# Last block of a two-layer hybrid network: scan's rows transposed between two products, masks signalled by chunk, last pass added and stored by halves

## The reference

```python
x = x + _L1_ffn_ref(_layernorm(x), w_gate, w_up, w_down)
x = x + _L1_attn_b_ref(_layernorm(x), W_act, W_val, W_rec)
x = x + _L1_ffn_ref(_layernorm(x), w_gate, w_up, w_down)

def _L1_ffn_ref(x, w_gate, w_up, w_down):
    h = silu(x @ w_gate) * (x @ w_up)            # 1024 wide
    h_sparse = _sparsify_2to4(h)                 # of each 4 neighbours the 2 largest in magnitude stay
    return h_sparse @ w_down

def _L1_attn_b_ref(x, W_act, W_val, W_rec):      # "the scan"
    ct = concat([x shifted by one row, x])       # 512 wide
    z = sigmoid(relu(ct @ W_act.T))              # 256 numbers, read as 128 complex ones
    z = z / cummax(|z|)                          # running maximum over the rows
    kv = running complex product of z over the rows
    r = sigmoid(relu(ct @ W_rec.T))
    return (kv @ W_val.T) * r ** 4
```

## Time and profile before

| | |
|---|---|
| median of 3 runs | 1644.63 us (1636.43 to 1647.76) |
| the profiled execution's own time | 1641.78 us |
| its span, first to last instruction | 1639.7 us |
| TensorE matmuls busy | 1398.7 us, 85% of the span |
| VectorE busy | 1049.0 us, 64% |
| ScalarE busy | 625.2 us, 38% |
| GpSimd busy | 295.8 us, 18% |
| mean granted clock of TensorE | 0.924 of full |
| bytes moved by DMA | 42.00 MB, mean 26 GB/s |

### The profile page before, as it was taken

The page is one execution under the profiler, slowest core; times in us unless marked ns, Lnnn a source line. Parts: engine busy times, 40 slices in busy tenths (PEclk is TensorE's granted clock), DMA queues, the critical chain, the costliest instruction groups (busy, mean ns, idle before and its releaser), DMA issues. The chain is left out here.

```text
span 1639.7 us, 21649 instructions
## 1 busy us (share of the span) xinstructions
PE 1398.7 (85%) x8144; PEld 1002.1 (61%) x8144; DVE 1049.0 (64%) x2056; ACT 625.2 (38%) x1160; POOL 295.8 (18%) x251
## 2 busy tenths in 40 slices
PE   3799999857999877799976899898879979889897
PEld 2455555446888766688864444343257767677676
DVE  5555555187887456778746556666256568888775
ACT  1254544342333212333321455656632323433321
POOL 0210000044433200243331320200040200120010
PEclk9799999578999988999996799999989989999899
DMA  8615220040000000000015404110000000000000
GB/s 190 87 27 79 44 37 2 1 149 1 1 1 1 1 0 1 0 1 1 1 39 73 75 27 75 27 24 1 1 0 1 1 1 1 0 1 1 13 13 26
DMA packets 23063, 42.00 MB, mean 26 GB/s; under 512 B 4705, under 2 KB 6497, under 8 KB 22833
## 3 DMA queue, kind: packets, MB, share of 16 engines
q1 hardware_dynamic: 22960, 40.64, 13.2%
HBM read 14.54 MB, written 2.10 MB: 10 GB/s over the span
## 5 line engine op out<-in xcount | busy, mean ns | idle before, releaser
L1312 DVE TENSOR_REDUCE attn_negm<-ps 128x2 f32<-128x1024 f32 (+3 forms) x256 | 256.2, 1021 | 115.5 <-PE ps L940 57.4
L1160 ACT ACTIVATE attn_probs<-ps 128x512 f32<-128x512 f32 (+3 forms) x512 | 237.0, 515 | 188.9 <-PE ps L973 112.0
L480 POOL TENSOR_TENSOR moe_h_low<-moe_h,moe_h_high 128x512 fp32r<-128x512 f32 x96 | 139.8, 1458 | 328.8 <-ACT moe_h_high L430 328.8
L964 PE MATMUL ps<-attn_qs,attn_ks 64*128 64x512 f32 (+3 forms) x512 | 154.9, 418 | 38.1 <-ACT attn_probs L1160 35.4
L447 ACT ACTIVATE moe_silu<-ps 128x512 f32<-128x512 f32 x96 | 57.4, 598 | 228.0 <-PE ps L353 227.9
L940 PE MATMUL ps<-attn_ks,attn_qs 63*128 63x512 f32 (+3 forms) x512 | 120.9, 469 | 26.6 <-DMA attn_ks<-attn_part_low 21.5
L964 PEld LDWEIGHTS ps<-attn_qs,attn_ks 64*128 64x128 f32 x512 | 72.1, 193 | 102.7 <-ACT attn_probs L1160 97.9
L1683 PE MATMUL ps<-sb_f_down,tail_h 128*128 128x256 f32 x512 | 123.3, 387 | 7.1 <-DVEq L1976 7.1
L988 PE MATMUL ps<-attn_probs,attn_va 128*32 128x512 f32 (+3 forms) x1024 | 123.8, 559 | 0.0
L1683 PEld LDWEIGHTS ps<-sb_f_down,tail_h 128*128 128x128 f32 x512 | 98.5, 193 | 24.0 <-DVEq L1976 7.3
L940 PEld LDWEIGHTS ps<-attn_ks,attn_qs 63*128 63x128 f32 x512 | 51.9, 199 | 93.8 <-issue 62.4
(11 more groups left out here) (319 smaller groups left out, 3281.2 us busy)
## 6 DMA issues: line engine op xcount, KB each, us to landing
attn_qs<-attn_part_high SPq DMA_DIRECT2D x64, 128.0 KB, 4.9
attn_qs<-attn_part_low SPq DMA_DIRECT2D x32, 128.0 KB, 4.5
attn_ks<-attn_part_high SPq DMA_DIRECT2D x32, 128.0 KB, 6.1
attn_ks<-attn_part_low SPq DMA_DIRECT2D x16, 128.0 KB, 7.0
out_x<-x SPq DMA_DIRECT2D x4, 512.0 KB, 2.6
x<-in_x SPq DMA_DIRECT2D x1, 1536.0 KB, 12.9
attn_qs<-attn_mT SPq DMA_DIRECT2D x64, 4.0 KB
moe_raw<-in_f_gate SPq DMA_DIRECT2D x2, 512.0 KB, 6.3
```

The costliest lines, as they stand in the source:

```text
L480: pool.tensor_tensor(hc.low[:, j % RING, :], h[:, j % RING, :], hc.high[:, j % RING, :], ALU.subtract).then_inc(low_done, 1)
L964: last = pe.matmul(ps[:, SC + k, 0:width2(kt)], ks[e:e + ROWS2, b % 2, key_tile(hd), kt * P:(kt + 1) * P], qs[e:e + ROWS2, b % 2, hd // 2, ...
L1160: act.activation(pr[:, s2 % RING, j, 0:n], ps[:, SC + k, 0:n], ACT.Exp, scale=HD ** -0.5).then_inc(exp_done, 1)
L1312: dve.tensor_reduce(m, ps[:, 2 * half:2 * half + 2, 0:width1(qt)], AX, ALU.max, negate=True).then_inc(r1_free, 1)
```

## The change

Four edits, all in the last block.

1. **The scan's rows.** TensorE transposes the rows of entry b in slot s + 2 between `chunk(s + 2)` and `down(s - 5)`; before it did so at the end of slot s + 1. ScalarE's two copies move from the jobs of slot s + 1 to those of slot s + 2. The table `pe_between` is new. Banks stay as they were, since no other job of banks 6 and 7 lies in between.
2. **Masks by chunk.** `sel_done` and the instruction that signalled it are gone. down(m) waits for the count of VectorE's selection steps: 8 of the 11 steps of its four chunks for the first of them, then 9, 10 and 11.
3. **The last pass.** ScalarE's sum of pass 7 is gone. In down(63) each of the four row tiles signals, and VectorE adds bank 4 to x when two tiles are done and bank 5 when four are, straight from PSUM, 128x512 each.
4. **The last store.** Batch entry 3 is stored in two pieces of 256 KB, each behind its half of the addition.

```diff
@@ -1487,6 +1487,7 @@
     DOWN_LAG = 7
     SLOTS = CHUNKS + DOWN_LAG + 2
     DOWN = 4
+    SELECT = 11
     S1 = 8
     NS = T // S1
     TREE = [1 << k for k in range((NS - 1).bit_length())]
@@ -1497,22 +1498,23 @@
     def scan_from(b):
         return added(b)
 
-    pe_at, act_at, pool_at, dve_at, dve_first = ([[] for _ in range(SLOTS)] for _ in range(5))
+    pe_between, pe_at, act_at, pool_at, dve_at, dve_first = ([[] for _ in range(SLOTS)] for _ in range(6))
     for p in range(1, B):
         pe_at[FC * p - 4] += [("row", "f", p, c) for c in range(DC)]
         act_at[FC * p - 4] += [("row", "f", p, c) for c in range(DC)]
         dve_at[FC * p - 4] += [("row", "f", p, c) for c in range(DC)]
         pool_at[FC * p - 6].append(("normalise", "f", p))
     dve_at[0].append(("stats", "rest"))
-    for p in range(PASSES):
+    for p in range(PASSES - 1):
         act_at[added(p) - 1].append(("sum", p))
         dve_first[added(p)].append(("add", p))
+    dve_first[added(PASSES - 1)].append(("add", "last"))
     for b in range(B):
         s = scan_from(b)
         dve_first[s].append(("stats", "s", b))
         pool_at[s].append(("normalise", "s", b))
-        pe_at[s + 1] += [("row", "s", b, c) for c in range(DC)]
-        act_at[s + 1] += [("row", "s", b, c) for c in range(DC)]
+        pe_between[s + 2] += [("row", "s", b, c) for c in range(DC)]
+        act_at[s + 2] += [("row", "s", b, c) for c in range(DC)]
         pe_at[s + 2] += [("act", b, 0), ("act", b, 1)]
         act_at[s + 2] += [("act", b, 0), ("act", b, 1), ("square", b)]
         dve_at[s + 3] += [("sum", b), ("peak", b)]
@@ -1540,7 +1542,7 @@
 
     jobs = Turns([6, 7])
     early = [("row", "f", 0, c) for c in range(DC)]
-    for todo in [early, *pe_at]:
+    for todo in [early, *(between + after for between, after in zip(pe_between, pe_at))]:
         for job in todo:
             jobs.take(job, "dve" if job[0] == "out" or job[:2] == ("row", "f") else "act")
 
@@ -1570,7 +1572,7 @@
 
         gate_ready, up_ready = s.sem("gate_ready"), s.sem("up_ready")
         silu_done, prod_done, mag_done = s.sem("silu_done"), s.sem("prod_done"), s.sem("mag_done")
-        ge_done, sel_done = s.sem("ge_done"), s.sem("sel_done")
+        ge_done, tile_done, half_added = s.sem("ge_done"), s.sem("tile_done"), s.sem("half_added")
         down_done, x_done, x_scanned = s.sem("down_done"), s.sem("x_done"), s.sem("x_scanned")
         sum_done, totals_done, sel_steps, stored = s.sem("sum_done"), s.sem("totals_done"), s.sem("sel_steps"), s.sem("stored")
         w_high, w_low, consts = s.sem("w_high"), s.sem("w_low"), s.sem("consts")
@@ -1593,10 +1595,14 @@
 
         @block.sync
         def _(sp):
-            for b in range(B):
+            for b in range(B - 1):
                 sp.wait_ge(x_done, B + b + 1)
                 sp.dma_start(out[:, NT * b:NT * (b + 1), :], x[:, NT * b:NT * (b + 1), :]).then_inc(stored, 16)
-            sp.wait_ge(stored, 16 * B)
+            for half in range(2):
+                t0 = NT * (B - 1) + 2 * half
+                sp.wait_ge(half_added, half + 1)
+                sp.dma_start(out[:, t0:t0 + 2, :], x[:, t0:t0 + 2, :]).then_inc(stored, 16)
+            sp.wait_ge(stored, 16 * (B + 1))
 
         @block.tensor
         def _(pe):
@@ -1678,11 +1684,14 @@
                 p, j = m // FC, m % FC
                 if j == 0:
                     at_least(pe, sum_done, p)
-                pe.wait_ge(sel_done, m // QUAD + 1)
+                pe.wait_ge(sel_steps, SELECT * (m // QUAD) + SELECT - QUAD + m % QUAD + 1)
                 for t in range(NT):
                     last = pe.matmul(ps[:, DOWN + t // 2, (t % 2) * D:(t % 2 + 1) * D], h[:, j, t * P:(t + 1) * P], w_down[:, j, :],
                                      start=j == 0 and t % 2 == 0, stop=j == FC - 1, skip_group_check=True)
-                last.then_inc(down_done, 1)
+                    if m == CHUNKS - 1:
+                        last.then_inc(tile_done, 1)
+                if m < CHUNKS - 1:
+                    last.then_inc(down_done, 1)
 
             pe.wait_ge(g["arrived"]["scan"], g["loads"]["scan"])
             pe.wait_ge(g["arrived"]["ffn1"], g["loads"]["ffn1"])
@@ -1691,6 +1700,8 @@
             for n in range(SLOTS):
                 if n < CHUNKS:
                     chunk(n)
+                for job in pe_between[n]:
+                    do(job)
                 if 0 <= n - DOWN_LAG < CHUNKS:
                     down(n - DOWN_LAG)
                 for job in pe_at[n]:
@@ -1828,7 +1839,7 @@
 
         @block.vector
         def _(dve):
-            c = Chain(dve, sel_steps, 11)
+            c = Chain(dve, sel_steps, SELECT)
             cx = Chain(dve, scan_steps, 4 * (S1 - 1 + len(TREE) + 1))
 
             def row(kind, k, c):
@@ -1923,6 +1934,8 @@
                     row(*a)
                 elif kind == "stats":
                     stats(*a)
+                elif job == ("add", "last"):
+                    add_last_to_x()
                 elif kind == "add":
                     add_to_x(*a)
                 elif kind == "sum":
@@ -1973,7 +1986,13 @@
                         c.do(dve.scalar_tensor_tensor(hr, cnt[:, r, :], level, hr, op, ALU.mult))
                     c.sync()
                     c.end()
-                    dve.sem_inc(sel_done, 1)
+
+            def add_last_to_x():
+                for k in range(2):
+                    dve.wait_ge(tile_done, 2 * k + 2)
+                    t0 = NT * (B - 1) + 2 * k
+                    xk = x[:, t0:t0 + 2, :]
+                    dve.tensor_tensor(xk, xk, ps[:, DOWN + k, :].rearrange("p (t d) -> p t d", t=2), ALU.add).then_inc(half_added, 1)
 
             def add_to_x(p):
                 dve.wait_ge(sum_done, p + 1)
```

## The result

The changed kernel has a median of 1657.63 us (1651.61 to 1663.68) against 1647.06 us (1636.43 to 1660.4) for the kernel before, 22 runs each. The ratio is 1.0063 with a 95% interval of 1.0042 to 1.0084. That is 10.4 us slower, with 6.9 to 13.8 as the interval. The forecast was +7.3 us and 1651.9. The measured median lies 5.7 us above that time: 2.4 of it because the kernel before has a median of 1647.06 over these 22 runs and not 1644.63, and the rest, about 3, is the 10.4 against the 7.3, which lies within the interval.

The account below looks back on a forecast made before the run. TensorE's last-block idle time, mainly waits for `tail_xns` (16.3 us) and the selection (7.1), was taken as the limit. Terms -4.2 + 14.7 + 6.6 - 7.8 - 2.0 = +7.3 us on 1644.63 gave 1651.9, range 1642 to 1662.

Parts of the forecast that it names:

- the row copies held behind `tail_zt`: ScalarE's slot s + 2, entries 1 to 3: row copies wait behind the previous entry's `tail_zt` copies, together +14.7 us.
- first mask wait: TensorE's first wait for the selection falls from 2.94 to 1.1 us and the clock stays up: -3.5 us.
- transposes: Entry 0's scan start: the chunk fills TensorE's wait, so the act products start 4.2 us earlier.
- copies: Late row copies in ScalarE's queue start the act products 4.3, 5.0 and 5.4 us later for entries 1, 2, 3.
- middle mask wait: TensorE's third selection wait, 0.7 us, goes away: -0.7 us.
- clock: Act products of entries 1 to 3 run partly at half speed after TensorE idles 9.7 us: +2.2 us each, +6.6 together.
- last mask wait: TensorE's last selection wait falls from 3.51 to 1.6 us and the matmuls behind it run faster: -3.6 us.
- end: After the last matmul: one half's addition from PSUM (-1.6 us) and a smaller last store (-0.4), together -2.0 us.
- The rival in which the clock doesn't come back: After each of three long TensorE waits the clock stays low, costing 11.9 us each: +29.1 us, 1681.0; chance 0.06.
- The rival that had the delay swallowed at the next scan start: Existing `tail_xns` waits at entries 2 and 3 absorb up to 4.8 us each: -2.3 us, 1642.3; chance 0.10.

Follow-up runs that it names:

- part 1 alone: The kernel before with only the scan-row transposes and ScalarE's two row copies moved to slot s + 2: 1670.23 against 1646.38 us, ratio 1.0130.

## Why the prediction was right

The forecast was +7.3 us with the time at 1651.9; the block shows +7.6, and the runs +10.4 with an interval that holds both. The mechanism that it named, the row copies held behind `tail_zt`, is the one that the runs show. By its own steps, each from start to start of the act products (the starts lie 87.75, 155.32, 217.59 and 279.49 us into the block before, 79.46, 151.61, 221.14 and 290.07 after):

| stretch | terms of the forecast | forecast | measured |
|---|---|---|---|
| up to entry 0's act products | first mask wait -3.5, transposes -4.2 | -7.7 | -8.3 |
| entry 0 to 1 | copies +4.3, middle mask wait -0.7 | +3.6 | +4.6 |
| entry 1 to 2 | copies +5.0, clock +2.2 | +7.2 | +7.3 |
| entry 2 to 3 | copies +5.4, clock +2.2 | +7.6 | +7.0 |
| entry 3 to the end | clock +2.2, last mask wait -3.6, end -2.0 | -3.4 | -3.0 |
| sum | | +7.3 | +7.6 |

The stretches miss by up to 1.0 us, in both directions, and nearly cancel. That the sum is right to 0.3 is luck. That each stretch is right to 1.0 is what the mechanism gave.

*The copies behind `tail_zt`.* Shown in three ways: by the row of ScalarE above, by the one line that moves the copies ahead, and by the one number that moves them late in the kernel before. The act products of entries 0, 1 and 3, which answer to the earlier trace rows:

```profile
1286.86 5.32 PE L1628 MATMUL ps<-tail_xs,sb_s_act 128*128 128x512 f32 x12
...
1359.01 2.90 PE L1628 MATMUL ps<-tail_xs,sb_s_act 128*128 128x512 f32 x3 [9.61 <-ACT tail_xs L1720]
...
1497.46 2.90 PE L1628 MATMUL ps<-tail_xs,sb_s_act 128*128 128x512 f32 x3 [9.68 <-ACT tail_xs L1720]
```

Entry 0 has no wait ahead of them, entries 1 and 3 have 9.61 and 9.68 us; the forecast's length was 9.7.

*The clock.* Busy time by stretch over the act products of entries 1 to 3, the granted clock third from the end:

```profile
1359.01:1368.45 9.44, 9.44 (x17) 4.21 (x18) 2.32 (x3) 0.60 (x1) 0.00 (x0) 0.75 0.01 2
1428.54:1437.35 8.81, 8.81 (x17) 3.92 (x18) 2.26 (x3) 0.60 (x1) 0.00 (x0) 0.81 0.00 0
1497.46:1507.64 10.18, 10.18 (x17) 4.41 (x18) 2.27 (x3) 0.60 (x1) 0.00 (x0) 0.70 0.01 2
```

The kernel before, entry 2:

```profile
1420.37:1427.40 7.03, 7.03 (x18) 3.19 (x17) 6.86 (x13) 0.91 (x3) 0.00 (x0) 1.00 0.00 0
```

The losses are 2.4, 1.8 and 3.2 us, together 7.3 where the sum had 6.6 and the bounds 4.4 and 8.7. The last is beyond the 2.9 that the forecast gave a single wait. Three waits of one length in one execution were followed by 4.7, 3.4 and 6.2 us at the lower level. The Trainium skill (TensorE: Matmul & The Clock Gate, What's actually happening) says that the number of slow matmuls is not the same in every run of a kernel. The trace agrees and shows it for three restarts of one execution. The rival in which the clock doesn't come back did not happen.

*The masks.* The two waits that remain are 1.09 and 1.62 us, forecast 1.1 and 1.6, and the clock stayed up after both. The 32 matmuls of the last four downs took 7.17 instead of 8.80 us. The term of 0.7 for the middle wait was wrong: that wait is gone, but TensorE only came earlier to the next one, for entry 1's `tail_xns`, which VectorE and GpSimd set. It lasted 1.57 us in the changed kernel, and 1.09 with part 1 alone, where the middle wait stands; 3.83 - 2.74 = 1.09 is also what the forecast's own terms give. So the stretch from entry 0 to entry 1 grew by 4.6 us and not by 3.6.

*The delay handed on.* VectorE's waits from the act products of entry 1 to those of entry 3, before and after:

```profile
DVE tail_h L1949 <- ACT tail_silu L1789: 11.6, 4, 3.8
```

```profile
DVE tail_h L1962 <- ACT tail_silu L1800: 25.4, 4, 10.5
```

They grew by 13.8 us while the stretch grew by 14.3: VectorE stood idle for nearly all of the delay, and none of it was made up at the next start. Each cycle is longer by the full copies and clock terms. The rival that had the delay swallowed at the next scan start (-2.3 us) fell.

*The end.* The changed kernel, which answers to the last rows and to the earlier trace rows:

```profile
1641.53 7.17 PE L1689 MATMUL ps<-sb_f_down,tail_h 128*128 128x256 f32 x32 [1.62 <-DVE tail_h L1986]
1647.95 1.48 DVE L1995 TENSOR_TENSOR x<-x,ps 128x512 f32<-128x512 f32 x2 [4.67 <-PE ps L1689]
1648.66 1.12 SPq L1604 DMA_DIRECT2D out_x<-x  x2
```

```profile
out_x<-x SPq DMA_DIRECT2D x2, 256.0 KB, 2.0
```

The second half's addition ended at 1649.43, 0.7 us behind the last matmul's end at 1648.70, where it was 2.3. The last store landed in 2.0 us instead of 2.6. Together 2.2 us, forecast 2.0. The Trainium skill (DMA: Bandwidth & Descriptors, Anatomy of one DMA) would have some 2.3 us for 256 KB, an estimate by its fixed 2.0 and half of what 512 KB took beyond it. That section gives the 2.0 for transfers issued by GpSimd, and these stores are issued by SyncE. The store of 256 KB took what the 128 KB load of the earlier trace rows took, so the measurement is a little under the estimate.

## What to carry to other kernels

When a job moves to a later slot, look at every queue that it stands in and not only at the one that was waiting: here TensorE's part moved by one chunk as meant, while ScalarE's part moved behind a copy that waits for another engine's last step. The wait ahead of such a neighbour costs nothing as long as what stands behind it is in no hurry, and the trace of before shows its length. A scheme that puts producer and consumer into one slot needs the copy between them ahead of everything in that slot that waits.

## What the runs showed that was not expected

The masks by chunk gave 13.1 us alone where 7.8 were forecast, and a part of the surplus lies where two engines work at the same time. GpSimd normalises the four row groups of entry 0 while VectorE comes to its three comparisons. The second profile of the kernel before, GpSimd and then VectorE:

```profile
1286.13 5.28 POOL L1812 TENSOR_SCALAR tail_xns<-x,tail_ns_minus,tail_ns_rstd 128x256 f32<-128x256 f32 x4
```

```profile
1287.65 3.49 DVE L1958 TENSOR_TENSOR tail_ge<-tail_mag 128x1536 bf16<-128x1536 f32 x3
```

And with the masks by chunk alone:

```profile
1286.22 3.73 POOL L1813 TENSOR_SCALAR tail_xns<-x,tail_ns_minus,tail_ns_rstd 128x256 f32<-128x256 f32 x4
```

```profile
1287.85 3.78 DVE L1959 TENSOR_TENSOR tail_ge<-tail_mag 128x1536 bf16<-128x1536 f32 x3
```

GpSimd's fourth row group took 3.66 us in the first and 2.13 in the second, against 0.56 for the others. In the first it started 0.09 us after VectorE's first comparison and ended 0.26 us after the last one. In the second it started 0.02 us ahead of the first comparison and ended 0.34 us after that one, and VectorE lost 0.29 us over its three comparisons. All profiles of this case fall into these two kinds: the five with the masks as before have the late start (by 0.08 to 0.09 us) and 3.66 to 3.67 us, the six with masks by chunk have the early one (by 0.01 to 0.02) and 2.13 to 2.14.

The Trainium skill (SBUF — State Buffer, SBUF: two separate sides) describes a pair of ports that VectorE and GpSimd share as a lock. A VectorE instruction with two inputs in SBUF takes it against a GpSimd instruction that reads SBUF, and the one that starts first has it for the whole instruction. The comparisons have two such inputs. The first kind agrees with that for the first comparison; that GpSimd waited through three on end goes beyond what the page says. The second kind doesn't agree on who goes first: by its start GpSimd was ahead, and still it took 2.13 us and not 0.56. A tenth of a us in the order of two starts went with 1.5 us here. No run changed it by itself: that shared ports are the reason is argued from the rows and not shown.
